# Cross-attention with 1601 keys: the 65 keys over twelve chunks dealt 17, 16, 16, 16 over four row groups, four exponentials over marked banks, chunks turned 3, 4, 4, 2

## The reference, cut to what matters

```python
# query: (32, 64, 256); key_in and value: ctx_1024, (32, 1601, 256)
q = jnp.einsum('bsd,df->bsf', query, Wq) + bq
k = jnp.einsum('bsd,df->bsf', key_in, Wk) + bk
v = jnp.einsum('bsd,df->bsf', value, Wv) + bv
attn = jnp.einsum('bqd,bkd->bqk', q, k)
probs = jax.nn.softmax(attn, axis=-1)
result = jnp.einsum('bqk,bkd->bqd', probs, v)
x = result + query
...
return (x - mu) * jax.lax.rsqrt(var + LN_EPS) * gamma + beta
```

## Time and profile before

| | |
|---|---|
| median of 3 runs | 531.81 us (531.1 to 534.37) |
| the profiled execution's own time | 533.65 us |
| its span, first to last instruction | 531.9 us |
| PE busy, share of the span | 497.1 us, 93% |
| DVE busy | 399.8 us, 75% |
| ACT busy | 200.0 us, 38% |
| turning of the context on DVE (L1663), 128 of 1008 ns | 121.7 us |
| score matmuls (L1135), 2048 | 93.8 us busy |
| weighted-sum matmuls (L1159), 832 | 93.6 us busy |

### The profile page before, as it was taken

How to read it: one execution, slowest core, us unless ns; L and a number is a source line. 1 busy time by engine, 2 the same in 40 slices (tenths; PEclk the granted TensorE clock), 3 DMA queues, 4 the chain that set the end, 5 groups by cost and what they waited for, 6 DMA issues and landing times.

```text
span 531.9 us, 14446 instructions
## 1 busy us (share of the span) xinstructions
PE 497.1 (93%) x5012; PEld 347.7 (65%) x5013; DVE 399.8 (75%) x1080; ACT 200.0 (38%) x617; POOL 198.1 (37%) x314
## 2 busy tenths in 40 slices
PE   7998999999999999999989999999998979999990
PEld 6665656656666666666655667766754658888860
DVE  3799699999899999899663488898775515555764
ACT  2343413433223333332312466665431035555510
POOL 4000412212221122112221667676776605666640
PEclk9999999999999999999999999999998979999996
DMA  7999579877998788885314899810122235555747
GB/s 280 362 359 265 185 266 304 259 201 251 296 309 281 269 275 273 259 269 204 98 41 128 264 291 310 251 52 2 41 80 91 90 99 150 159 155 154 223 116 221
DMA packets 67604, 108.83 MB, mean 205 GB/s; under 512 B 8371, under 2 KB 49381, under 8 KB 67560
## 3 DMA queue, kind: packets, MB, share of 16 engines
q1 hardware_dynamic: 61144, 97.83, 58.9%
q0 software_dynamic: 3792, 8.43, 4.5%
q10 hardware_dynamic: 2624, 1.97, 1.2%
HBM read 85.31 MB, written 24.85 MB: 207 GB/s over the span
## 4 chain that ended last, share of the span: by engine, by line
PE 71%; DVE 9%; DMA 8%; POOL 5%; issue 4%; ACT 1%; SPq 1%; POOLq 0%; DVEq 0%; ACTq 0%
PE banks L1135 15%; PE banks L1159 15%; PE banks L1541 8%; DMA ring<-in_ctx_dram 4%; POOL rows_by_expert L752 4%; PE banks L1553 4%; PE banks L1147 3%; DVE ctxT L1663 3%; PE banks L1172 3%; PE banks L1094 2%; PE banks L1535 2%; PE banks L1268 2%; PE banks L1320 2%; PE banks L1180 2%; PE banks L1275 2%
## 5 line engine op out<-in xcount | busy, mean ns | idle before, releaser
L1663 DVE STREAM_TRANSPOSE ctxT<-ring 128x832 f32<-128x832 f32 x128 | 121.7, 1008 | 4.4 <-DMA ring<-in_ctx_dram 4.4
L1135 PE MATMUL banks<-ctxT,qT_all 32*64 32x416 f32 (+2 forms) x2048 | 93.8, 498 | 1.6 <-issue 0.9
L1159 PE MATMUL banks<-ring,prob 128*64 128x256 f32 (+1 forms) x832 | 93.6, 381 | 0.7 <-ACT prob L864 0.7
L1159 PEld LDWEIGHTS banks<-ring,prob 128*64 128x64 f32 (+1 forms) x832 | 58.6, 137 | 31.5 <-issue 4.2
L1135 PEld LDWEIGHTS banks<-ctxT,qT_all 32*64 32x64 f32 x2048 | 56.8, 131 | 30.3 <-issue 13.0
L663 POOL TENSOR_TENSOR var<-mv,eps 128x1 f32<-128x1 f32 x32 | 6.3, 196 | 167.7 <-DVE mv L1708 115.6
L786 POOL DMA_INDIRECT expert_out<-prob,dest x47 | 46.2, 984 | 41.7 <-DVE prob L2124 26.1
L877 ACT ACTIVATE prob<-banks,negmax 128x416 f32<-128x416 f32 (+2 forms) x80 | 41.1, 531 | 30.2 <-DVE negmax L1685 30.2
L1541 PE MATMUL banks<-ring,ctxT 128*128 x188 | 50.7, 394 | 0.1
L699 POOL TENSOR_TENSOR ctxT<-ctxT,k_mask 128x1088 f32<-128x1088 f32 x16 | 33.1, 2068 | 25.3 <-ACT ctxT L955 25.3
L864 ACT COPY prob<-banks 128x512 f32<-128x512 f32 x64 | 27.6, 514 | 38.3 <-PE banks L1147 38.2
(11 more groups left out here) (271 smaller groups left out, 940.0 us busy)
## 6 DMA issues: line engine op xcount, KB each, us to landing
ring<-in_ctx_dram SPq DMA_DIRECT2D x48, 1024.0 KB
qT_all<-q_by_pair SPq DMA_DIRECT2D x56, 128.0 KB, 8.9
rows_by_expert<-blank SPq DMA_DIRECT2D x8, 774.0 KB, 5.9
ctxT<-rows_by_expert SPq DMA_DIRECT2D x47, 129.0 KB, 2.1
mid<-stage SPq DMA_DIRECT2D x31, 128.0 KB, 2.3
ring<-in_ctx_dram SPq DMA_DIRECT2D x16, 130.0 KB
ctxT<-mid SPq DMA_DIRECT2D x16, 128.0 KB, 3.7
qT_all<-mid SPq DMA_DIRECT2D x16, 128.0 KB, 3.8
```

The source lines that it names most:

```text
L1135: last = pe.matmul(S[a][64 * b:64 * b + 64, 0:KW[a]], q_rep[mine, r, c, 64 * b:64 * b + 64], ctxT[mine, c, b, 0:KW[a]], start=c == 0, stop ...
L1159: last = pe.matmul(U[64 * b:64 * b + 64, 0:D], probT[0:rows, k, 64 * b:64 * b + 64], ring[0:rows, r, b, k, :], start=k == 0, stop=k == KT)
L1663: dve.transpose(ctxT[:, c].rearrange("p b (k j) -> p (b k) j", j=Q), ring[:, r].rearrange("p b k c -> p (b k) c")[:, :, columns(c):columns ...
```

## The change

Four things change together.
- The 65 last keys lie 17, 16, 16, 16 on the first rows of the four row groups (partitions 0, 32, 64 and 96 on), not on partitions 0 to 64. `KW` becomes 401, 400, 400, 400. SP loads them by four transfers.
- The thirteenth chunk is then full of gaps. `turn_probs`, `turned_out` and `weigh` handle it as 128 rows; the gaps of the context are zero.
- The scores' banks S[0] to S[3] are marked: DVE sets columns KW[a] to 415 of each to -1e30 once, at its start, after a wait that stood behind the first eight blocks. `exps` runs over all 416 columns of each bank, four instructions, and the marked columns give 0. Bank 0 also takes the first part of the turned probabilities, which must leave the marks alone.
- The parts of chunks become 3, 4, 4 and 2. The last part of a context load is chunk 11 alone (rows of 1 KB), followed by the four pieces of the tail, all after the last `pv_done`.

```diff
+    TAILS = [TAIL // QUADS + (1 if a < TAIL % QUADS else 0) for a in range(QUADS)]
+    KW = [KT * Q + n for n in TAILS]
+    NEVER = -1e30
-    KPARTS = [range(lo, min(lo + KG, KT + 1)) for lo in range(0, KT + 1, KG)]
+    KPARTS = [range(0, 3), range(3, 7), range(7, 11), range(11, KT + 1)]
+    CTX_LOADS = 16 * (len(KPARTS) + QUADS)
...
             def load_part(i, r, g):
...
+                lo, hi = KPARTS[g][0], min(KPARTS[g][-1] + 1, KT)
+                sp.dma_start(ring[:, r, :, lo:hi, :].rearrange("p b k c -> p b (k c)"),
+                             pair[:, 0:KT * P, :].rearrange("b (p k) c -> p b k c", k=KT)[:, :, lo:hi, :]
+                             .rearrange("p b k c -> p b (k c)")).then_inc(ctx_loaded[r], 16)
+                if hi == KT:
+                    for a, n in enumerate(TAILS):
+                        at = KT * P + sum(TAILS[:a])
+                        sp.dma_start(ring[Q * a:Q * a + n, r, :, KT, :],
+                                     pair[:, at:at + n, :].rearrange("b p c -> p b c")).then_inc(ctx_loaded[r], 16)
...
             def turned_out(i):
...
-                    rows = P if ks[0] < KT else TAIL
-                    act.copy(probT[0:rows, ks[0]:ks[-1] + 1, :].rearrange("p a b -> p (a b)"),
-                             PT_BANKS[g][0:rows, 0:len(ks) * P]).then_inc(probT_copied, 1)
+                    act.copy(probT[:, ks[0]:ks[-1] + 1, :].rearrange("p a b -> p (a b)"),
+                             PT_BANKS[g][:, 0:len(ks) * P]).then_inc(probT_copied, 1)
...
             def exps(i):
...
-                for n, (a, lo, hi) in enumerate(EXPS):
...
-                    act.activation(to, of, ACT.Exp, bias=negmax[:, 0:1], accum_out=sums[:, n:n + 1]).then_inc(exp_done, 1)
+                for a in range(QUADS):
+                    act.activation(by_slab[:, :, a, :], S[a][:, 0:SLAB].rearrange("p (k j) -> p k j", j=Q), ACT.Exp,
+                                   bias=negmax[:, 0:1], accum_out=sums[:, a:a + 1]).then_inc(exp_done, 1)
...
+            dve.wait_ge(bk_row_copied, 1)
+            for a in range(QUADS):
+                dve.memset(S[a][:, KW[a]:SLAB], NEVER)
             for c in range(BLOCKS):
                 block_turned(0, 0, c, 0)
             x_statistics(1)
-            dve.wait_ge(bk_row_copied, 1)
```

More of the change, by code:

```diff
@@ L28, in perceiver_layer @@
     SLAB = (KT + 1) * Q
-    KW = [KT * Q + max(0, min(Q, TAIL - Q * a)) for a in range(QUADS)]
-    EXPS = [(a, lo, hi) for a in range(QUADS) for lo, hi in ((0, KW[a] // Q * Q), (KW[a] // Q * Q, KW[a])) if lo < hi]
-    KG = 4
+    TAILS = [TAIL // QUADS + (1 if a < TAIL % QUADS else 0) for a in range(QUADS)]
+    KW = [KT * Q + n for n in TAILS]
+    NEVER = -1e30
     EARLY = 5
-    KPARTS = [range(lo, min(lo + KG, KT + 1)) for lo in range(0, KT + 1, KG)]
+    KPARTS = [range(0, 3), range(3, 7), range(7, 11), range(11, KT + 1)]
+    CTX_LOADS = 16 * (len(KPARTS) + QUADS)
     LN_EPS = 1e-5
@@ L166, in perceiver_layer @@
         negmax = sb("negmax", [P, 1])
-        sums = sb("sums", [P, len(EXPS)])
+        sums = sb("sums", [P, QUADS])
         rowsum = sb("rowsum", [P, 1])
@@ L1139, in turn_probs @@
             def turn_probs(i, first=False):
-                pe.wait_ge(exp_done, (i + 1) * len(EXPS))
+                pe.wait_ge(exp_done, (i + 1) * QUADS)
                 for g, ks in enumerate(KPARTS):
@@ L1145, in turn_probs @@
                     for a, k in enumerate(ks):
-                        rows = P if k < KT else TAIL
-                        last = pe.transpose(PT_BANKS[g][0:rows, a * P:a * P + P], prob[:, k * P:k * P + rows], ident[:, :])
+                        last = pe.transpose(PT_BANKS[g][:, a * P:a * P + P], prob[:, k * P:k * P + P], ident[:, :])
                     last.then_inc(probT_done, 1)
@@ L1156, in weigh @@
                     for k in ks:
-                        rows = P if k < KT else TAIL
                         for b in range(2):
-                            last = pe.matmul(U[64 * b:64 * b + 64, 0:D], probT[0:rows, k, 64 * b:64 * b + 64],
-                                             ring[0:rows, r, b, k, :], start=k == 0, stop=k == KT)
+                            last = pe.matmul(U[64 * b:64 * b + 64, 0:D], probT[:, k, 64 * b:64 * b + 64],
+                                             ring[:, r, b, k, :], start=k == 0, stop=k == KT)
                     last.then_inc(pv_done, 1)
@@ L1661, in block_turned @@
                 if c == 0:
-                    dve.wait_ge(ctx_loaded[r], round_ * 16 * len(KPARTS) + 16 * len(KPARTS))
+                    dve.wait_ge(ctx_loaded[r], round_ * CTX_LOADS + CTX_LOADS)
                 dve.transpose(ctxT[:, c].rearrange("p b (k j) -> p (b k) j", j=Q),
@@ L1687, in row_sum @@
             def row_sum(k):
-                dve.wait_ge(exp_done, (k + 1) * len(EXPS))
+                dve.wait_ge(exp_done, (k + 1) * QUADS)
                 dve.tensor_reduce(rowsum[:, :], sums[:, :], AX.X, ALU.add).then_inc(rowsum_ready, 1)
```

5 lines of the change are left out of this document (removed).

## The result

The changed kernel takes 538.45 us (median of 4 runs, 535.36 to 541.22) against 532.34 for the kernel before, run beside it (4 runs): a ratio of 1.0089, with a 95% interval of 1.0051 to 1.0128. It is slower, above the forecast range (528 to 537) and about where rival 4 stands with half of the turns late (537.5).

A forecast was written before the change was run, and what follows sets the result against it. TensorE was taken to set the pace, DVE following closely. Scores -2.8, exponentials -0.2, start +1.2 and steady loads +1.3 summed to -0.5 us, from 531.81 to 531.3 us; range 528 to 537.

The forecast's parts named there:

- rival 4: Context loads land later than their margins and lengthen the turns: 544.1 us, or 537.5 with half as many late; chance 0.17.
- the last of the loads: Steady cross-attention turns: later context loads make DVE wait in some turns, +1.3 us in all, bounds 0 and 9.6.
- The delay of a load: Each context load lands 1.6 us later, from chunk 11's 1 KB rows and the 17-row piece; bounds 0.35 to 2.1.
- The start: DVE's wait for the first context load: the delay is paid in full, +1.2 us, bounds 0.35 and 2.1.
- The scores: Score matmuls on PE: longest width falls from 416 to 401, 0.19 us a pair over 15 pairs, -2.8 us.
- Exponentials and marks: ACT: four exponentials of 606 ns, -0.2 us in pair 0; four DVE memsets, some 0.5 us, hidden by first load: 0.
- rival 2: Loads stay hidden except at the start (+0.35 us): 529.2 us, or 528.9 if all of a half-block scales; chance 0.2.
- rival 3: No gain in PE, because mean width or instruction issue sets the scores' pace; costs as forecast: 534.1 us; chance 0.13.

The follow-up runs named there:

- the merged load: Chunk 11 loaded with chunks 7 to 10 in one transfer: on the changed kernel 537.78 us, with its 17-row piece also split into 16 and 1, 534.88 us.
- The best version: Changed kernel with the 17-row piece split into 16 and 1, chunk 11 loaded with chunks 7 to 10, stores from ACT's queue: 531.29 us, ratio 0.9962.

## Why the prediction was wrong

**The step that failed** is the last of the loads: "Of the 13 turns I let one lose 1 us more [...] and reckon 0.3 us for the others together", +1.3 us. Six turns grew, together +5.04, and with the 0.17 us that each should have gained the loads cost about 6.1 us; DVE's waits for loads went from 0.9 to 6.2 us. The margin was mis-sized. I had read 2.7 us in one turn, from when the engines as a whole ran dry, with the queries' bytes taken as the last to pass. The steps of the load's semaphore show pair 11 landing at 188.16 us, not at about 187, so even this turn had 189.66 - 188.16 = 1.5 us. The median over pairs 8 to 15 is 1.3, the smallest margins are 0.5 us and none. My own delay of 1.6 us and a turn 0.2 us shorter would have used up nearly all of them. The 6.1 us lie between the term and its bound for margins of typically 1 us, 9.6. Part of the reason for the thin margin is the store between the freed slot and the load; it stood in the trace of before, though not in the lines of the earlier trace rows.

**The delay of a load** (1.6 us, bounds 0.35 to 2.1) was too small by 0.6 us, just outside its bounds: a load takes 13.75 us from its first issue to its landing, before 11.52. The larger part was rightly put on the 17 rows (1.1 to 1.4), and chunk 11's 0.35 agrees with the 0.2 to 0.4 in the table, as far as the merged load can tell. What was put at nothing is the number of small transfers ("SP's own issues are no bound"): on the kernel before it costs 0.6 to 0.8 us.

**The start** (+1.2, bounds 0.35 and 2.1): +1.94 at the first block and at the maxima (26.49 to 28.44), +1.75 at the scores of pair 1. The 0.2 between them is the shorter exponentials, as forecast.

**The scores** (-2.8): the size was right, 5.74 to 5.56 us, at 498 ns a matmul. In the turns it is paid out at 0.12 to 0.19 us. "DVE has that much spare" was true just so: in the clean turn shown the maxima wait 0.45 us for PE at 129.82, in the next one they start without a wait (144.09), and PE's weight loads wait for DVE's last blocks 18 times, 3.6 us in all, instead of 3 times, 0.7. The next microsecond will probably have to come out of DVE too.

**Exponentials and marks**: four of 609 ns, as forecast. The four memsets take 0.14 us together, not 0.5 and less than the lower bound of 0.3; they start at 14.50, as the copy of bk_row ends 0.8 us later than in before, and are done long before the load comes. The term 0 was right.

**The rivals.** 4 happened, at about half its strength, and my own test stood in the text: it decides from a mean DVE wait of 0.2 us a turn and passes 1% at 0.5. The mean wait was 6.2 / 13 = 0.48. The best version comes out about where rival 2 put the change, but with edits that the change did not have; rival 3 is refuted. The chance of 0.17 for rival 4 was too small beside a measured negative margin and a delay of 1.6 us.

## What to carry to other kernels

Where a load's margin matters, read it in every turn, not in one: the time from the slot's release to the load's issue, and from its landing to its use. Take the landing from the load's own semaphore, not from when the engines fall idle. Look at what stands ahead of the load in its queue; a store that waits for a result hands its delay on to the next load (here the first part went out 5.0 us after the weighted sum began, and 1.7 us with the store elsewhere). And if a small load has to be cut, try its partition rows at 16, not at 17, which here cost 1.1 to 1.4 us a load; the uncut 65 rows were no worse than any cut.

## What the hardware showed that I had not expected

- One row more in a small transfer, 17 for 16 (34 KB of 3.28 MB a pair), makes the whole load land 1.1 to 1.4 us later: over pairs 8 to 15 a load of after ends on 14 to 34 packets of 1 KB that pass one at a time, with 16 + 1 rows on at most 2. The cut into 16 + 1 took about 4 us off after.
- Four more small transfers with the same bytes make a load land 0.6 to 0.8 us later (11.5 us to 12.1 and 12.3).
- 256 rows of 1 KB instead of 5 KB rows cost nothing measurable in the device time: 538.45 and 537.78 us, and 534.62 and 534.88. The load lands 0.2 to 0.4 us later.
- With four row groups at work, widening one of them from 401 to 416 columns takes the scores of a pair from 5.56 to 5.73 us, as much as two groups at 416 and two at 384 and 385 (5.74).
